# An attention block and a four-way Mamba scan on one core: three of sixteen scan inputs made on ScalarE in a turned layout

## What is computed

```
theta = x @ w_theta                     # 256 pixels x 8
phi   = maxpool2x2(x @ w_phi)           # 64 x 8
g     = maxpool2x2(x @ w_g)             # 64 x 32
attn  = softmax(theta @ phi.T)          # 256 x 64
x     = x + sigma * (attn @ g @ w_o + b_o)
```

```
hs, gate = split(rmsnorm(x) @ W_in.T)
u   = silu(causal_conv4(hs) + conv_b)
dt  = softplus(dt_r @ W_dt.T + b_dt);  Bm, Cm, dt_r from u @ W_x.T
state[n] = exp(dt * A[n]) * state[n] + dt * u * Bm[n]      # for n in 0..15, step by step
y   = sum_n state[n] * Cm[n] + u * Dp
out = rmsnorm(x + (y * silu(gate)) @ W_out.T)
```

## Time and profile before

| | before |
|---|---|
| median of 3 runs | 887.56 us (885.71 to 888.86) |
| the profiled execution | 886.92 us, its span 885.1 us |
| mean granted TensorE clock | 0.983 |
| busy share of the span: PE, DVE, ACT, POOL | 91%, 93%, 67%, 93% |
| HBM traffic | 291 GB/s over the span |

### The profile page before, as it was taken

How to read it: one execution, slowest core, us unless ns; L and a number is a source line. 1 busy time by engine, 2 the same in 40 slices (tenths; PEclk the granted TensorE clock), 3 DMA queues, 4 the chain that set the end, 5 groups by cost and what they waited for, 6 DMA issues and landing times.

```text
span 885.1 us, 8939 instructions
## 1 busy us (share of the span) xinstructions
PE 803.1 (91%) x2208; PEld 358.6 (41%) x2208; DVE 827.6 (93%) x633; ACT 588.9 (67%) x798; POOL 819.9 (93%) x377
## 2 busy tenths in 40 slices
PE   8599999999999899999999989999999999998685
PEld 5244334443434344343434434344443444443232
DVE  2699999999999999999999999999999999999992
ACT  4585866859577594957759585775858668584331
POOL 0699999999999999999999999999999999999980
PEclk9899999999999999999999999999999999999997
DMA  1698998888899988888898989888888989888960
GB/s 50 248 341 287 332 309 300 309 302 310 296 327 301 331 272 322 320 293 313 309 330 277 326 300 312 297 313 322 301 285 336 316 290 322 315 290 304 327 237 3
DMA packets 78051, 258.35 MB, mean 292 GB/s; under 512 B 13104, under 2 KB 15408, under 8 KB 78000
## 3 DMA queue, kind: packets, MB, share of 16 engines
q1 hardware_dynamic: 78000, 257.79, 83.2%
HBM read 254.60 MB, written 3.15 MB: 291 GB/s over the span
## 4 chain that ended last, share of the span: by engine, by line
DVE 32%; DMA 18%; issue 16%; POOL 15%; ACT 14%; PE 3%; SPq 1%; DVEq 0%; POOLq 0%; ACTq 0%
DVE ps_x L1071 11%; DMA c_all<-bc_dram 8%; DMA b_all<-bc_dram 8%; DVE state L1071 8%; POOL inp L914 8%; DVE state L1078 8%; POOL state L920 6%; ACT ps_x L755 4%; ACT L729 3%; DVE state L1064 3%; ACT L726 2%; DVE yg L1086 2%; ACT u L722 2%; DMA bc_dram<-bc_rows 1%; PE ps_y L557 1%
## 5 line engine op out<-in xcount | busy, mean ns | idle before, releaser
L914 POOL TENSOR_TENSOR inp<-du,b_all 128x1024 f32<-128x1024 f32 x224 | 524.0, 2355 | 13.9 <-DVE ps_x L1071 13.0
L557 PE MATMUL ps_y<-state,packed 128*128 128x512 f32 x1024 | 475.9, 603 | 23.4 <-POOL state L920 23.3
L755 ACT ACTIVATE ps_x<-step,a_neg 128x1024 f32<-128x1024 f32 x224 | 249.7, 1115 | 132.5 <-DVE state L1071 60.5
L1071 DVE TENSOR_TENSOR_SCAN ps_x<-ps_x,inp 128x1024 f32<-128x1024 f32 x144 | 327.1, 2283 | 8.7 <-ACT ps_x L755 3.5
L557 PEld LDWEIGHTS ps_y<-state,packed 128*128 128x128 f32 x1024 | 188.7, 191 | 263.8 <-issue 199.2
L920 POOL TENSOR_TENSOR state<-state,c_all 128x1024 f32<-128x1024 f32 x112 | 263.8, 2355 | 4.9 <-DVE state L1071 3.0
L1071 DVE TENSOR_TENSOR_SCAN state<-ps_x,inp 128x1024 f32<-128x1024 f32 x80 | 179.2, 2272 | 2.1 <-issue 1.2
L1078 DVE TENSOR_TENSOR state<-ps_x,c_all 128x1024 f32<-128x1024 f32 x144 | 172.5, 1213 | 6.7 <-issue 6.4
L1064 DVE TENSOR_TENSOR_SCAN state<-decay,ps_x 128x1024 f32<-128x1024 f32 x32 | 72.9, 2278 | 0.3 <-ACT decay L762 0.2
L542 PE MATMUL ps_x<-u,w_b_wide 128*128 128x512 f32 x128 | 63.4, 618 | 6.3 <-DVE state L1078 5.8
L466 PE MATMUL ps_w<-xpad,w_conv 128*128 128x512 f32 x128 | 61.8, 606 | 3.2 <-ACT ocen L785 3.0
(11 more groups left out here) (119 smaller groups left out, 603.1 us busy)
## 6 DMA issues: line engine op xcount, KB each, us to landing
c_all<-bc_dram SPq DMA_DIRECT2D x256, 512.0 KB, 5.6
b_all<-bc_dram SPq DMA_DIRECT2D x224, 512.0 KB, 6.0
xt<-in_x_t SPq DMA_DIRECT2D x32, 64.0 KB, 5.4
bc_dram<-bc_rows SPq DMA_DIRECT2D x32, 64.0 KB, 2.7
out<-ofin SPq DMA_DIRECT2D x16, 64.0 KB, 5.9
packed<-in_packed SPq DMA_DIRECT2D x1, 635.0 KB, 4.2
packed<-in_packed SPq DMA_DIRECT2D x1, 129.0 KB, 2.2
w_qkv<-in_w_qkv SPq DMA_DIRECT2D x1, 64.0 KB, 2.0
```

What stands on the lines that cost most here:

```text
L557: last = mm(ps_y[:, HALF * half:HALF * (half + 1)], ident, state[n % H_RING][:, HALF * half:HALF * (half + 1)], start=(n == 0), stop=(n == ...
L755: f(ps_x[n % 2][:, :], step[b.buf][:, :], ACT.Exp, scale=a_neg[:, n:n + 1]).then_inc(ps_decay_done, 1)
L914: tt(inp[i % IN_RING][:, :], du[b.buf][:, :], b_all[i % B_RING][:, :], ALU.mult).then_inc(pool_inputs, 1)
L1071: v.tensor_tensor_scan(held if KIND[n] == "P" else x, x, inp[i % IN_RING][:, :], 0.0, ALU.mult, ALU.add).then_inc(scans, 1)
```

## The change

`KIND` becomes "ACCPACCCCPACPPCC": states 0 and 4, which were "D", and state 10, which was "P", become "A". The scan input of an "A" state is made in turned layout, where pixels lie on partitions, so that Bm of a pixel is a per-partition scalar. Once per image PE turns the rows of B and C (`bt_turn`, four 128 x 128 turns) and `du` (`dut_turn`, eight turns in two halves), and ACT copies them out (`bt_copy`, `dut_copy`). For each "A" state ACT makes eight 128 x 128 copies with `scale=bt` (`act_input`), PE turns them back into `ps_x` (`turn_input`, eight turns), and the scan reads decay from SBUF and input from PSUM as a "D" scan did. The multiplication on DVE, the spread by PE, and the load of Bm and POOL's multiplication for state 10 go; its decay moves from `ps_decay` to `sb_decay`.

The softmax's division goes from DVE to ACT: `exp(-ln(sum))`, then two copies with a scale. The residual is folded into `attn_out`: `xa` holds the turned attention on partitions 0 to 63 and x on 64 to 127, and `gw` holds an identity on the lower half, so one matmul does both. The gate is stored in two pixel orders, and `gated` becomes two instructions. The hand-written orders of all engines are changed with it.

```diff
-KIND = "DCCPDCCCCPPCPPCC"
+KIND = "ACCPACCCCPACPPCC"
-                sp.dma_start(xt[C * half:C * half + C, :], a["x_t"][j.num, :, :]).then_inc(x_loaded, 16)
+                sp.dma_start(xa[POOLED:, :], a["x_t"][j.num, :, :]).then_inc(x_loaded, 16)
...
-                    last = mm(attn_bank(j)[:, 128 * k:128 * (k + 1)], attn[:, k, :], ident,
-                              start=True, stop=True)
+                    last = nc.tensor.transpose(attn_bank(j)[:, 128 * k:128 * (k + 1)], attn[:, k, :], ident)
...
-                mm(attn_bank(j)[:, L:2 * L], gw[:, :], attn_t[:, :], start=True, stop=False)
-                mm(attn_bank(j)[:, L:2 * L], ident, xt[:, :], start=False, stop=True).then_inc(o_done, 1)
+                mm(attn_bank(j)[:, L:2 * L], gw[:, :], xa[:, :], start=True, stop=True).then_inc(o_done, 1)
...
-            def spread_b(b, n):
...
+            def bt_turn(j):
+                pe.wait_ge(bc_rows_done, j.num + 1)
...
+                for k in range(HALF // 128):
+                    last = nc.tensor.transpose(w0[:, 128 * k:128 * (k + 1)], bc_rows[:, 128 * k:128 * (k + 1)], ident)
+                last.then_inc(bt_ps, 1)
+            def dut_turn(j, half):
+                pe.wait_ge(du_done, j.num + 1)
+                at_least(pe, dut_done, 2 * j.num + half)
+                for k in range(TURNS // 2):
+                    at = HALF * half + 128 * k
+                    last = nc.tensor.transpose(w1[:, 128 * k:128 * (k + 1)], du[j.buf][:, at:at + 128], ident)
+                last.then_inc(dut_ps, 1)
+            def turn_input(b, n):
+                i = act_in_index(b, n)
+                pe.wait_ge(a_scaled, i + 1)
...
+                at_least(pe, *x_free_wait(b, n - 2))
+                for k in range(TURNS):
+                    last = nc.tensor.transpose(ps_x[n % 2][:, 128 * k:128 * (k + 1)], scaled[i % A_RING][:, k, :], ident)
+                last.then_inc(a_turned, 1)
...
+                f(eln[:, :], esum[:, :], ACT.Ln).then_inc(eln_done, 1)
...
+                f(erec[:, :], eln[:, :], ACT.Exp, scale=-1.0).then_inc(erec_done, 1)
...
+                for k in range(CHUNKS):
+                    last = f(attn[:, k, 0:POOLED], attn_bank(j)[:, POOLED * k:POOLED * (k + 1)], ACT.Copy,
+                             scale=erec[:, k:k + 1])
...
-                f(gate[j.buf][:, :], w0[:, 0:L], ACT.Silu).then_inc(gate_done, 1)
+                for d in range(2):
+                    f(grid(gate[j.buf][:, d, :]), ordered(w0[:, 0:L], d), ACT.Silu).then_inc(gate_done, 1)
...
+            def act_input(b, n):
+                i = act_in_index(b, n)
+                act.wait_ge(dut_done, 2 * (b.num + 1))
+                act.wait_ge(bt_done, b.num + 1)
+                at_least(act, a_turned, i - A_RING + 1)
+                for k in range(TURNS):
+                    half, at = k // (TURNS // 2), k % (TURNS // 2)
+                    row = 2 * N * half + n
+                    last = f(scaled[i % A_RING][:, k, :], dut[b.buf][:, k, :], ACT.Copy,
+                             scale=bt[b.buf][:, at, row:row + 1])
+                last.then_inc(a_scaled, 1)
...
-                for d in range(DIRS):
-                    v.tensor_tensor(grid(yg[:, d, :]), ordered(ps_y[:, L * d:L * (d + 1)], d), grid(gate[j.buf][:, :]),
-                                    ALU.mult).then_inc(yg_done, 1)
+                for e in range(2):
...
+                    v.tensor_tensor(yg[:, 2 * e:2 * e + 2, :].rearrange("p d (h w) -> p d h w", h=SIDE),
+                                    ps_y[:, HALF * e:HALF * (e + 1)].rearrange("p (d h w) -> p d h w", d=2, h=SIDE),
+                                    turned, ALU.mult).then_inc(yg_done, 1)
```

More of the change, by code:

```diff
@@ L20 @@
 CHUNKS = L // 128
+TURNS = T // 128
 EPS = 1e-5
@@ L130, in build @@
         u = [sb(f"u_{q}", [I, T]) for q in range(2)]
-        gate = [sb(f"gate_{q}", [I, L]) for q in range(2)]
+        gate = [sb(f"gate_{q}", [I, 2, L]) for q in range(2)]
         step = [sb(f"step_{q}", [I, T]) for q in range(2)]
         du = [sb(f"du_{q}", [I, T]) for q in range(2)]
-        bc_rows = sb("bc_rows", [4 * N, HALF])
+        bc_rows = sb("bc_rows", [128, HALF])
+        bt = [sb(f"bt_{q}", [128, HALF // 128, 4 * N]) for q in range(2)]
+        dut = [sb(f"dut_{q}", [128, TURNS, I]) for q in range(2)]
+        scaled = [sb(f"scaled_{q}", [128, TURNS, I]) for q in range(A_RING)]
         decay = [sb(f"decay_{r}", [I, T]) for r in range(D_RING)]
@@ L299, in load_weights @@
             def load_weights():
-                for half in range(2):
-                    sp.dma_start(xt[C * half:C * half + C, :], a["x_t"][0, :, :]).then_inc(x_loaded, 16)
+                sp.dma_start(xa[POOLED:, :], a["x_t"][0, :, :]).then_inc(x_loaded, 16)
                 sp.dma_start(w_qkv[:, :], a["w_qkv"]).then_inc(qkv_weights_in, 16)
@@ L655, in steps @@
                     attn_turn(later)
+                if done:
+                    out_final(done)
                 if coming:
-                    spread_b(coming, 0)
+                    turn_input(coming, 0)
                 if later:
@@ L932, in prologue @@
                 scan_input(first, 7)
-                product(first, 3)
             def finish(j):
@@ L956, in steps @@
                     scan_input(coming, 2)
+                    product(coming, 0)
                     scan_input(coming, 3)
-                    product(coming, 0)
                     scan_input(coming, 5)
@@ L961, in steps @@
                     scan_input(coming, 7)
-                    product(coming, 3)
             program(pool, prologue, steps, finish)
@@ L985, in attn_setup @@
                 v.tensor_tensor(sigma_b[:, :], w("sigma"), w("b_o"), ALU.mult).then_inc(sigma_b_done, 1)
+                for half in range(2):
+                    v.tensor_copy(gw[POOLED:, C * half:C * (half + 1)], ident[POOLED:, C:2 * C]).then_inc(gw_set, 1)
             def conv_setup():
@@ L1112, in prologue @@
                 row_max(second)
-                attn_norm(second)
                 first_bc(first)
-                scan_input(first, 0)
             def finish(j):
```

272 lines of the change are left out of this document (148 added, 124 removed).

## The result

The changed kernel takes **854.22 us** (median of 4 runs, 852.12 to 855.99); the kernel before took 886.63 us beside it (883.96 to 888.86). The ratio is 0.9649, with a 95% interval of 0.962 to 0.9679. The forecast was 862 us, with 855 to 872 as its own range and 847 to 893 over all cases; the result lies 0.8 us under the first and inside the second. The profiled execution took 855.12 us, its span 852.9.

The account below looks back on a forecast made before the run. DVE and POOL were taken to fill an image's 51.84 us together; 15 x (51.84 - 50.0) = 27.6, + 2 - 4 = 25.6 less than 886.92 gives 861.3, with 0.6 to the median 862 us; range 855 to 872.

Parts of the forecast that it names:

- Both engines bind, so both reliefs count together: DVE and POOL both fill an image's 51.84 us; the change takes 2.74 off DVE and 2.30 off POOL.
- DVE's floor: DVE's work per image without two multiplications, the division and 0.09 of the gate: 51.84 - 2.74 = 49.1 us.
- POOL's 49.5: POOL's time per image without one of 22 multiplications, keeping its short waits: 51.84 - 2.30 = 49.5 us.
- Period after 50.0: Time per image after the change: DVE's 49.1 plus stalls of 0.7 and 0.2, 50.0 us, above POOL's 49.5.
- First place: ACT before `hid_squares`: state 10's eight copies, 2.0 us, are just hidden by the 1.97 wait for `hid_proj`.
- Second place: PE before the scan of state 4: its input waits behind the convolution, stalling DVE 0.9 or 0.3; 0.7 taken.
- Third place: Softplus before state 9's decay: ACT needs 8.1 us where DVE has 7.85 us of work, a stall of 0.2.
- Rival A: Turns at 0.295 make PE the bound: period 54.7, 932 us; decides from about 0.22 a turn; chance 0.15.
- The 275 ns: The skill's time for one PE-mode transpose; by it 36 turns were estimated at 9.9 us, PE's load at 53.0.
- Rivals B and C: B: ACT's order binds, 880 us, chance 0.18; C: freed time returns as waits, no effect, 887 to 892 us, 0.11.
- an image takes 51.84 us: Period before the change, read in DVE's timeline between scans of state 4 at 413.35 and 465.19.
- The start: Before the first scan: turns and copies make it 4.3 us later; 4 counted, as POOL makes inputs ahead.

Follow-up runs that it names:

- the two kernels with one relief: Changed kernel with state 10 back on POOL, 883.7 us; changed kernel with states 0 and 4 back on DVE, 887.89 us; each with fitting lists.
- the run at 0.224: Changed kernel with its 36 turns per image for scan inputs made by ordinary matmuls with the identity: 885.6 us, ratio 1.0001.

## Why the prediction was right, and where a step failed

- **Both engines bind, so both reliefs count together**: right, and shown by the two kernels with one relief. DVE's floor was forecast at 49.1; 49.39 less its two stalls is 49.0. POOL's 49.5 was a little high: periods of 49.39 occur.
- **Period after 50.0**: right; the mean over 14 is 49.87. That it came out so close is partly luck: the stalls were over-sized, 0.38 in place of 0.9, and the 14 periods are on the mean 0.48 longer than the image shown, which was not forecast.
- **First place, the copies before `hid_squares`**: right. Here is ScalarE's timeline there:

```profile
442.14 2.43 ACT L834 ACTIVATE scaled<-dut,bt 128x128 f32<-128x128 f32 x8
444.48 0.57 ACT L842 ACTIVATE hsq<-ps_w 128x512 f32<-128x512 f32 x1
```

  The wait of 1.97 before the squares is gone, and its total fell from 42.1 us to 9.4. The cover was used up to the end: eight copies take 2.34, 0.293 each, where 0.25 was forecast. The gap between two unlike instructions was too small a price. The Trainium skill, "ScalarE: Activation LUTs", section "What ACT_TABLE_LOAD costs", gives an instruction 186 ns and 0.833 ns a column, 93 more for a pointer operand, and an overlap of 93 back to back; by an estimate from it that is 293 ns for 128 columns. The trace agrees.
- **Second place, PE before the scan of state 4**: the right place, with 0.18 in place of 0.7; the part was forecast as late and is just in time. The forecast had the convolution wait for `hln` on ACT. In the trace `hln` ends at 448.43, and PE comes to the convolution at 448.64 with its list full since 444.24, so what is left of the stall is PE's own work.
- **Third place, softplus before state 9**: 0.20, as forecast. The profile names no releaser, but ACT's decay of that state, behind softplus and a table load, runs from 417.02 to 418.14, and the scan starts at 418.22.
- **Rival A, turns**: its mechanism is real. Its point of decision was a turn of 0.22, with PE's 51.0 and 1 us of waits making 52.0; the run at 0.224 has 51.43 and 51.87, and the time of before. What it had wrong was the price. The 0.295 came from two turns alone; in a run of eight the same ordinary turn takes 0.224, so 0.14 of those 0.59 us is no turn's. The weight loads at 0.11 were the nearer row for the new kind, which takes 0.125. The transposing turns cost 36 x 0.125 = 4.5 us, of 5.3 forecast.
- **The 275 ns** of the Trainium skill, "TensorE: Matmul & The Clock Gate", Part 4 (PE-mode transpose), agree with the row of the profile's page: 278 ns is the mean duration here, in fp32, where that section gives its figure beside one for bf16. The estimate of 9.9 us made of it counted a duration where starts 0.125 apart count. Its rule on the clock changed nothing in the middle, where the granted clock is 1.00.
- **Rivals B and C** fell. ACT is busy 46.4 of 50 us, as forecast (46.0 a period), and DVE's waits for its decays are 4.9 us in the whole span.
- **The failed step** is "an image takes 51.84 us", read between two scans of state 4. The mean of 14 periods before was (815.32 - 84.97) / 14 = 52.17: several images were over 52, up to 53.3. That is 14 x 0.33 = 4.6 of the 6.6 us by which the sum was too small; the after period gives 14 x 0.13 = 1.8. In those 14 periods VectorE waits seven times before a product with a row of C, 4.6 us in sum, and the image read has no such wait. The profile names no releaser, but the chain that ended last leads to the longest of them through a load of such a row:

```profile
481.25 7.12 DMA c_all<-bc_dram
488.37 1.14 issue
489.51 1.24 DVE state L1078
```

  So the loads, which the prediction had binding on neither side, are the likely cause; no run tested it. The rest nearly cancels: the first scan came 6.5 us later in place of 4 net, and the first image gave back 4.4 in place of 1.8.
- **The start** was under-sized for one more reason. Here is TensorE's timeline ahead of the first scan:

```profile
34.83 1.97 PE L572 MATMUL ps_x<-packed,scaled 128*128 128x128 f32 x8 [3.16 <-ACT scaled L834]
36.59 1.06 PE L452 MATMUL ps_x<-xa,gw 128*128 128x256 f32 x2
```

  The eight turns take 1.76 from start to start, where they take 1.00 in the middle. The window from 34.80 to 36.60 shows the granted clock (0.50) during them:

```profile
34.80:36.60 1.80, 1.77 (x9) 1.78 (x10) 0.00 (x0) 1.80 (x5) 0.00 (x0) 0.50 1.04 376
```

  That is the lower level, 1.2 GHz. PE had waited for POOL and ACT before; it was busy 2.17 us between 30 and 36 us, at a mean granted clock of 0.56, and 2.82 us between 24 and 30, at 1.00.

## What to carry over

When two engines fill the period together, an edit that relieves one can be worth next to nothing and look like a failed idea; price both floors and relieve both, with the third engine's floor in the same sum. Price a short instruction by the distance of starts in a run of its own kind and not by its duration or by a pair of them, and read the period over many images, not one. When you undo a part to test it, give the lists of all engines the order that fits, or the test measures the order.

## What was not expected of the hardware

- A turn in transpose mode is one instruction and takes 0.125 us of PE in a run of eight, 0.224 for the ordinary fp32 matmul's two instructions; the durations shown, 278 ns on the mean, overlap.
- With 36 turns an image among the matmuls the granted clock stayed at 1.00 in all seven middle windows that were read, from 60 to 750 us.
- With more places for rows of B, a row's 512 KB landed 7.6 us after its issue in place of 6.6 (medians), at a DMA share of 0.9, and the time can't be told from that of the changed kernel.
